# One-core tower of token mixer, linear attention and eight experts: attention by single rows in laps, its later steps set beside the experts, heads set in the layers

## The reference

```python
h = tok(x)      # embedding, decayed running sum over the sequence, norm;
                # 4 layers: x += gelu(LN(x) @ W1 + b1) @ W2 + b2   (128 -> 512 -> 128)
                # head: h = x @ head_W + head_b                    (128 -> 64)
h = h + attn(layernorm(h))
    # xn = rmsnorm(x); q, k, v = xn @ w_qkv (4 heads of 32)
    # q = softmax over the head's 32; k = softmax over the sequence and 4 memories
    # context = k v^T (32x32 a head); out = rmsnorm(context q @ w_out + b_out) + x
h = h + ffn(layernorm(h))
    # xn = LN(x); logits = xn @ Wr + br; top 2 of 8 experts, w = softmax of the two
    # y = sum over experts of w[e] * (gelu(xn @ W1[e] + b1[e]) @ W2[e] + b2[e])
```

## Time and profile before

| | |
|---|---|
| median of 3 runs | 480.24 us |
| profiled execution | 481.16 us, span 479.4 us |
| PE, DVE, ACT, POOL busy | 87%, 76%, 69%, 59% of the span |
| last matmul of the layers ends | 246.4 us |
| heads on PE | 249.3 to 262.1 us |
| last turn of attention begins | 343.0 us |
| first spread of gates | 381.5 us |
| last sum transposed | 474.5 us |

### The profile page before, as it was taken

How to read it: one execution, slowest core, us unless ns; L and a number is a source line. 1 busy time by engine, 2 the same in 40 slices (tenths; PEclk the granted TensorE clock), 3 DMA queues, 4 the chain that set the end, 5 groups by cost and what they waited for, 6 DMA issues and landing times.

```text
span 479.4 us, 6268 instructions
## 1 busy us (share of the span) xinstructions
PE 414.8 (87%) x1965; PEld 333.3 (70%) x1965; DVE 364.4 (76%) x925; ACT 328.8 (69%) x530; POOL 282.1 (59%) x416
## 2 busy tenths in 40 slices
PE   3765799999999999999999495959593989999995
PEld 2653678888888888887779384848472767777773
DVE  4996489999999999999849759697937756666662
ACT  1255588888888888888961534444463689999893
POOL 0267467777777777778005916464642066677763
PEclk9999799999999999999995768687675699999997
DMA  6700021221222222222000000000000000000000
GB/s 219 267 1 1 1 44 43 46 46 45 43 49 43 44 50 44 45 44 45 23 1 1 0 2 1 1 1 1 1 0 1 1 1 12 11 12 12 11 12 22
DMA packets 15833, 14.93 MB, mean 31 GB/s; under 512 B 9781, under 2 KB 10553, under 8 KB 15545
## 3 DMA queue, kind: packets, MB, share of 16 engines
q1 hardware_dynamic: 15800, 14.54, 12.8%
HBM read 13.42 MB, written 1.11 MB: 30 GB/s over the span
## 4 chain that ended last, share of the span: by engine, by line
PE 36%; DVE 32%; ACT 23%; POOL 4%; issue 4%; DMA 0%; POOLq 0%; SPq 0%; DVEq 0%; ACTq 0%
PE ps L1223 31%; DVE hid_lo L868 7%; ACT hid L562 7%; ACT hid_hi L567 6%; DVE stats L790 6%; DVE xn L858 6%; ACT xn_hi L558 4%; PE ps L1421 2%; DVE hh L1042 1%; DVE x L802 1%; PE ps L1534 1%; ACT x L600 1%; DVE x L809 1%; DVE st L1029 1%; POOL xn_hi L493 1%
## 5 line engine op out<-in xcount | busy, mean ns | idle before, releaser
L868 DVE TENSOR_TENSOR hid_lo<-hid,hid_hi 128x1024 fp32r<-128x1024 f32 x64 | 78.3, 1223 | 23.0 <-ACT hid_hi L567 23.0
L562 ACT ACTIVATE hid<-ps,b_fold 128x512 f32<-128x512 f32 x128 | 83.9, 682 | 15.9 <-PE ps L1223 15.8
L1223 PE MATMUL ps<-xn_hi,w_all 128*128 128x512 f32 x256 | 89.0, 409 | 0.9 <-DVE xn_lo L863 0.9
L1223 PE MATMUL ps<-hid_hi,w_all 128*128 128x512 f32 x256 | 84.1, 390 | 0.0
L567 ACT ACTIVATE hid_hi<-hid 128x1024 fp32r<-128x1024 f32 x64 | 67.9, 1061 | 2.0
L1198 DVE TENSOR_TENSOR hid<-hid,ps 128x512 f32<-128x512 f32 x64 | 43.8, 686 | 33.1 <-ACT hid L710 31.6
L1223 PEld LDWEIGHTS ps<-xn_hi,w_all 128*128 128x128 f32 x256 | 48.7, 190 | 12.8 <-DVE xn_lo L863 2.2
L1223 PEld LDWEIGHTS ps<-hid_hi,w_all 128*128 128x128 f32 x256 | 48.1, 188 | 10.3 <-DVE hid_lo L868 0.4
L1223 PE MATMUL ps<-xn_lo,w_all 128*128 128x512 f32 x128 | 50.4, 394 | 0.0
L1223 PE MATMUL ps<-hid_lo,w_all 128*128 128x512 f32 x128 | 49.8, 389 | 0.0
L710 ACT ACTIVATE hid<-ps,eb_fold 128x512 f32<-128x512 f32 x64 | 43.6, 686 | 8.1 <-PE ps L1223 7.5
(11 more groups left out here) (221 smaller groups left out, 890.9 us busy)
## 6 DMA issues: line engine op xcount, KB each, us to landing
rstd_row<-roots SPq DMA_DIRECT2D x29, 256.0 KB, 4.1
hh<-in_tokens SPq DMA_DIRECT2D x8, 256.0 KB, 8.1
hid<-in_w SPq DMA_DIRECT2D x2, 1024.0 KB, 9.0
out<-hh SPq DMA_DIRECT2D x8, 128.0 KB, 2.0
ew_raw<-in_expert_w SPq DMA_DIRECT2D x1, 512.0 KB, 9.5
roots<-rstd SPq DMA_DIRECT2D x29, 2.0 KB, 1.4
ew_raw<-in_expert_w SPq DMA_DIRECT2D x1, 256.0 KB, 9.4
cons<-in_constants SPq DMA_DIRECT2D x1, 233.0 KB, 2.7
```

The costliest lines, as they stand in the source:

```text
L562: act.activation(hid[:, j % 2, f, :], bank[f], ACT.Gelu, bias=b1_fold[:, j // B * F + f:j // B * F + f + 1]).then_inc(gelu_done, 1)
L868: dve.tensor_tensor(hid_lo[:, j % 2, 2 * p:2 * p + 2, :], hid[:, j % 2, 2 * p:2 * p + 2, :], hid_hi[:, j % 2, 2 * p:2 * p + 2, :].bitcast( ...
L1223: return pe.matmul(out, lhsT, rhs, start=start, stop=stop)
```

## The change

1. *Late weights in the layers.* The fold's matmuls go into the prologue (`late_folds`), ACT's gains and hi parts to the start of rows j = 5 to 19, DVE's lo parts to the end of rows j = 6 to 24; the zeroing of w_pad on POOL goes between two roots.
2. *Heads in the layers.* `head(0)` to `head(4)` stand in rows j = 27 to 31 on PE, with `head_out` and `head_moments` on DVE one row later, and the rest behind; the z of row 0 is made and transposed ahead of the last `down`. Two banks serve the heads instead of four.
3. *Attention by single rows in laps.* Lap m runs from -9 to 7; those from 0 on are the expert rows. In lap m row m+9 gets its products and exps, row m+8 its K transposes and context, row m+6 its Q transposes and attend, row m+5 its output norm and residual, row m+4 its expert z and router columns; pairs of rows get gates. q stays in x for all rows, mx_sb has 4 places, qT and ezf are tiles of their own.
4. *Z by tensor operations.* `z_of` and `expert_z` take the whole row (128x256) with broadcast mean and root instead of four pieces with scalars; POOL subtracts the mean for z.
5. *Router.* The sum of the two logit parts is made by PE (`logits` multiplies by the selection matrix), the top two for 2 rows at once (128x64), the gate weights by total and gap (4 operations), the factor 0.5 in ACT's copy.
6. *Experts.* Hidden units turn through 2 banks instead of 4 (the other two carry the laps' transposes and products); the steps of rows 4 to 7 stand between the units, on each engine at a fixed u = n % 8.

The diff, cut to its core (ACT's steps between the experts' units stand like PE's: `q_turned` u=1, `ez_hi` 2, `attended` 4, `expert_z_turned` 5, `logits_out` 7, `copy_gates` 3 or 7):

```diff
 HALF = B // 2
 W1_STEP = 6
-GATES_BANK = (4, 6, 7, 4, 7, 7, 7, 7)
-LOGITS_BANK = (0, 5)
-HEAD_BANK = (2, 3, 6, 7)
-Z_ROW = 4
+HEAD_BANK = (7, 6)
+HIDDEN_BANK = (0, 4)
+SPREAD_BANK = (2, 3)
+EARLY_HEADS = 5
...
+def turning_bank(lap):
+    return 1 if lap >= 0 else 4 * (lap % 2) + 2
+def product_bank(lap):
+    return 5 if lap >= 0 else 4 * (lap % 2) + 3
...
+            for m in range(FIRST_LAP, 0):
+                a = m - FIRST_LAP
+                if m + 5 >= 0:
+                    output_norm(m + 5, (m + 5) % 2)
+                if a + 2 < B:
+                    roots_of(a + 2)
+                    centred(a + 2)
+                if a + 1 < B:
+                    residual_base(a + 1)
+                if m + 5 >= 0:
+                    expert_norm(m + 5, (m + 5) % 2)
...
             for n in range(UNITS):
-                if n % E in LO_BY_POOL:
+                m, u = divmod(n, E)
+                if u == 0 and m + 5 < B:
+                    output_norm(m + 5, (m + 5) % 2)
+                if u in LO_BY_POOL:
                     hidden_lo(n)
+                if u == 6 and m + 5 < B:
+                    expert_norm(m + 5, (m + 5) % 2)
...
             for j in range(L * B):
+                if j == 5:
+                    projection_scale()
+                if j == 7:
+                    projections_hi()
+                if j in (9, 11):
+                    expert_scale((j - 9) // 2)
+                if j in (13, 15):
+                    first_layer_hi((j - 13) // 2)
+                if j == 17:
+                    second_layer_hi()
+                if j == 19:
+                    expert_bias_hi()
                 for f in range(F):
...
+            for m in range(FIRST_LAP, 0):
+                a, c = m - FIRST_LAP, m - FIRST_LAP - 1
+                if a < B:
+                    z_turned(a, a % 2)
+                if m == FIRST_LAP:
+                    act.preload_act_table(ACT.Exp)
+                if m == -1:
+                    act.preload_act_table(ACT.Gelu)
+                if c >= 0:
+                    k_turned(c, c % 2)
+                if m + 6 >= 0:
+                    q_turned(m + 6, m % 2)
+                if m + 4 >= 0:
+                    ez_hi(m + 4, m % 2)
+                if m == -1:
+                    gate(0)
+                if a < B:
+                    exp_k(a, a % 2)
+                if a + 1 < B:
+                    z_hi(a + 1, (a + 1) % 2)
+                if m + 6 >= 0:
+                    attended(m + 6, m % 2)
+                if a < B:
+                    exp_q(a, a % 2)
+                    copy_v(a, a % 2)
+                if m + 4 >= 0:
+                    expert_z_turned(m + 4)
+                    logits_out(m + 4)
+                if m == -1:
+                    copy_gates(0)
...
+                if j >= L * B - 4:
+                    head_out(j - (L * B - 4))
                 if j == 0:
                     x_lo(1)
                 h_lo(j, 0)
+                if j >= L * B - 4:
+                    head_moments(j - (L * B - 4))
                 if 0 < j < L * B - 1:
                     x_lo(j + 1)
                 h_lo(j, 1)
+                if j == 6:
+                    gate_rows()
+                if j == 8:
+                    output_weights()
+                if j == 10:
+                    projections_lo()
+                if j in (16, 18):
+                    first_layer_lo((j - 16) // 2)
+                if j == 20:
+                    second_layer_lo()
+                if j == 21:
+                    v = expert_bias_lo()
+                if j == 22:
+                    v = expert_bias_gap(v)
+                if j == 23:
+                    v = expert_bias_half(v)
+                if j == 24:
+                    expert_bias(v)
+                if j == L * B - 2:
+                    z_of(0, 0)
             residual(L * B - 2)
+            z_lo(0, 0)
+            head_out(4)
+            head_moments(4)
             residual(L * B - 1)
...
+            for m in range(FIRST_LAP, 0):
+                a, c = m - FIRST_LAP, m - FIRST_LAP - 1
+                if c >= 0:
+                    v_total = softmaxes(c, c % 2)
+                if m + 5 >= 0:
+                    output_moments(m + 5, (m + 5) % 2)
+                if m == -2:
+                    v = first_max(0)
+                if a < B:
+                    max_k(a, a % 2)
+                    negated(a % 2, own.n)
+                if m == FIRST_LAP:
+                    for b in range(5, B):
+                        head_out(b)
+                if a + 1 < B:
+                    z_of(a + 1, (a + 1) % 2)
+                if m + 4 >= 0:
+                    expert_z(m + 4, m % 2)
+                if m == -2:
+                    v = first_hot(0, v)
+                if m == -1:
+                    v = weights(0, v)
+                    gates_out(0, v)
+                if c >= 0:
+                    masked_context(c, c % 2)
+                if a < B:
+                    max_q(a, a % 2)
+                    sub_q(a, a % 2, own.n)
+                if a + 1 < B:
+                    z_lo(a + 1, (a + 1) % 2)
+                if m + 4 >= 0:
+                    expert_z_lo(m + 4, m % 2)
+                if c >= 0:
+                    scaled_m(c, c % 2, v_total)
+                if a < 3:
+                    head_moments(a + 5)
+                if m + 5 >= 0:
+                    scaled_output(m + 5, (m + 5) % 2)
+                    residual_moments(m + 5, (m + 5) % 2)
+                if m == -2:
+                    v = second_max(0, v)
+                    v = second_hot(0, v)
...
+                m, u = divmod(n, E)
                 if n < UNITS:
                     dve_job(n)
                 if 1 <= n <= UNITS and (n - 1) % E in LO_BY_DVE:
                     hidden_lo(n - 1)
-                if n % E == SKEW + 2 and n >= E:
-                    output(n // E - 1)
+                if u == 0 and m + 5 < B:
+                    output_moments(m + 5, (m + 5) % 2)
+                if u == 1 and m + 4 < B:
+                    expert_z(m + 4, m % 2)
+                if u == 3 and m + 4 < B:
+                    expert_z_lo(m + 4, m % 2)
+                if u == 4 and m + 5 < B:
+                    scaled_output(m + 5, (m + 5) % 2)
+                if u == 5 and m + 5 < B:
+                    residual_moments(m + 5, (m + 5) % 2)
+                if m % 2 == 0 and m < 6:
+                    if u == 2:
+                        v = first_max(m // 2 + 1)
+                    if u == 3:
+                        v = first_hot(m // 2 + 1, v)
+                    if u == 6:
+                        v = second_max(m // 2 + 1, v)
+                    if u == 7:
+                        v = second_hot(m // 2 + 1, v)
+                if m % 2 and m < 6:
+                    if u == 2:
+                        v = weights((m + 1) // 2, v)
+                    if u == 3:
+                        gates_out((m + 1) // 2, v)
+                if u == SKEW + 2 and n >= E:
+                    output(m - 1)
...
             for j in range(L * B):
                 if j + 3 < L * B:
                     turn(x[:, (j + 3) % B, :], x_ready, j + 4, j + (B + 3))
                 if j + 1 < SPREAD_BY_PE:
                     broadcast((j + 1) % 4, j + (B + 1))
                 up(j)
+                if j == L * B - EARLY_HEADS:
+                    pe.wait_ge(ld["headw"], 16)
+                    pe.wait_ge(normed, B + SPREAD_BY_PE + FREE)
+                if j == L * B - EARLY_HEADS + 1:
+                    pe.wait_ge(stats_ready, B * (L + 1) + FREE)
+                if j >= L * B - EARLY_HEADS:
+                    head(j - (L * B - EARLY_HEADS))
                 if j:
                     down(j - 1)
-            down(L * B - 1)
...
                 pe.wait_ge(zt_ready, b + 1)
+                if b >= 2:
+                    pe.wait_ge(m_ready, b - 1)
                 mm(kb, wqkv[:, 0, P:2 * P], zt[:, k, :], stop=False)
                 mm(kb, wqkv[:, 1, P:2 * P], zt[:, k, :], start=False).then_inc(k_done, 1)
+                wait_turned(turned)
+                wait_products(products)
...
+            head(5)
+            for m in range(FIRST_LAP, 0):
+                a, c = m - FIRST_LAP, m - FIRST_LAP - 1
+                turned_by_now, products_by_now = dict(turned), dict(products)
+                if 0 < a < B:
+                    z_transposes(a, a % 2)
+                if c >= 0:
+                    k_transposes(c, c % 2)
+                if m + 6 >= 0:
+                    pe.wait_ge(qsub_ready, c + 1)
+                    pe.wait_ge(v_ready, c + 1)
+                    q_transposes(m + 6, m % 2)
+                if m == -2:
+                    logits(0)
+                if a < B:
+                    qkv(a, a % 2, turned_by_now, products_by_now)
+                if m == FIRST_LAP:
+                    head(6)
+                    head(7)
+                    pe.wait_ge(h0_ready, B)
```

(54 more changed lines are left out.)

764 lines of the change are left out of this document (332 added, 432 removed).

## The result

The changed kernel takes 469.03 us (median of 5 runs, 467.92 to 476.24) where the kernel before takes 480.24 (479.58 to 484.65). The ratio is 0.9736, with a 95% interval of 0.9691 to 0.9781: 2.2 to 3.1% faster. The forecast was 456.5 with a range of 446 to 471, so direction and range hold, and the gain is 11.2 us where 23.8 stood. Its stages come out the same within 0.7 us in a second profile (experiment 1).

What follows compares the result with a forecast made beforehand. Bound: PE and an equal ACT-DVE chain in the layers, no full engine between, PE in the experts. 481.16 + 1.2 + 5.5 + 4.5 + 1.5 - 51.6 + 15.1 = 457.4 us profiled, 456.5 as median; range 446 to 471.

Steps and rivals of the forecast that it cites:

- Prologue, +1.2: Prologue: 18 small fold matmuls moved into PE's step 5 cost 1.2 us, bounds 0 and 2.3.
- Layers and heads, +5.5, +4.5, +1.5: Layers: DVE's weight splits and POOL's memset cost 5.5 us, five heads 4.5, z_transposes(0) ahead of the last down 1.5.
- the 263: Sign: last down of the layers at 259 us, right between 256 and 263; a layer end past 263 is wrong.
- Laps, 83.5: Between layers and experts: single-row laps take 83.5 us where 135.1 stood, -51.6, from 76.8 at full and 88.9 at half clock.
- The clock rival: Laps: every lap costs its half-clock length and the experts start cold, 464 us in all; chance 0.18.
- The experts, +15.1: Experts: PE's added steps, less gate transpositions already there, plus 5 us for stalls and the half-clock start: +15.1 us.
- PE's added steps: Experts: transpositions, attends, routes, logits and gates add 12.1 us to PE at full clock, less 2.1 already there.
- the 5: Experts: 5 us for stalls in rows 0 to 3 and the start at the half clock, bounds 0 and 12.
- DVE 13.3 against PE 14.6: Experts, row 0: busy sums of 14.6 us for PE, 13.3 for DVE, 12.7 for ACT, 10.7 for POOL.
- DVE and POOL slow each other: Laps and expert rows 0 to 3: DVE work beside POOL's gets longer, +7 and +6, 470 us; chance 0.1.
- Lock-step: Expert rows 0 to 3: two hidden banks make each unit a chain of 1.9 us, not 1.7; 467 us; chance 0.1.

Runs made afterwards that it cites:

- experiment 1: The changed kernel run again with no edit, for a second profile and time: ratio to the kernel before 0.9687 to 0.9848 (interval).
- ez_later: Changed kernel with PE's expert z transpositions at unit 5 instead of 4 and the route at unit 7 instead of 6: ratio 0.9634 to the kernel before.
- before_again: The kernel before, run again with no edit, for a second profile of its prologue: the layers began at 59.1 us; no total time given.
- ez_folds: ez_later with the prologue's late folds moved behind the first weight split and DVE's two additions ahead of the layers: ratio 0.9612 to the kernel before.
- ez_one_input: ez_later and one_input together on the changed kernel: 117.1 us from first spread to last sum in the experts; no total time given.
- one_input: Changed kernel with POOL's two-input subtraction for the hidden low halves replaced by a one-input multiplication, sums less exact: 465.56 us against 473.54 unedited.

## Why the prediction was right in sign and wrong in size

By its own terms, against the profiled executions:

*Prologue, +1.2.* 3.3 to 4.0. The bounds were 0 and 2.3, and the step failed where I took half of the 18 matmuls' time as hidden and nothing for what stands behind them. Even at the higher pace, where they take the 2.3 that I had, the layers begin 3.3 to 4.0 later, with the broadcast and transpositions behind them at the lower pace; at the lower pace the matmuls themselves take nearly twice as long.

*Layers and heads, +5.5, +4.5, +1.5.* In sum 11.5 forecast, 9.5 to 9.9 measured. Split: the memset 0.1 instead of 1.6, the experts' splits 2.2 instead of 2.7, which leaves 7.2 to 7.6 for heads, z transpositions and the other splits, where 7.2 stood. The layers' end is at 265, past the 263 that I had named as a sign of error, but that comes from the later begin, 62.2 instead of 54.3.

*Laps, 83.5.* 78.1 to 83.8 in twelve profiles, 81.4 in the first. The sum is right, and DVE as the bound of the later laps, but its parts erred in opposite ways: DVE is busy 66.9 us where the nine laps were to hold 70.9, at a granted clock of 0.84 where 0.72 was taken, and waits 14.6 where 12.6 was left. The clock rival (every lap at the half level) did not come.

*The experts, +15.1.* +31, and this step failed. Between the sums stand 17.4, 16.9, 17.0, 12.6, 13.5, 11.3 and 9.2 us, where I had 14.5, 14, 13, 12.5, 11.5, 11.5 and 11.0, and 26.1 from the first spread to the first sum instead of 17.0 before. The forecast was 10.0 for PE's added steps (12.1 - 2.1) and 5 for everything else: stalls and the start at the half clock. It is the 5 that failed; it measured 19.8.

(a) The added steps take 11.4, counted in the profile of `ez_later` from each start to the next and less the gate transpositions that stood there before. The logits are the piece that was mis-sized, 5.6 in all instead of 2.7: each pair needs 16 small instructions,

```profile
341.51 1.95 PE L1327 MATMUL ps<-cons,xn 16*128 16x8 f32 x16
```

where the kernel before had 8 transpositions a pair. A product with the selection matrix is an fp32 matmul, and shows as two instructions each. The other added steps take 5.7 where 7.3 stood.

(b) PE's own work in the experts is stretched. With the two moves of `ez_later`, near the full clock, PE is busy 106.6 against 88.8 (`before_again`), +17.8, which is 6.4 more than the added steps. Most of it stands in the matmuls with the experts' weights, the same in both kernels, at 0.99 and 1.00 of the clock; first `ez_later`, then `before_again`, those matmuls alone:

```profile
340.20:458.40 118.20, 78.50 (x253) 44.98 (x252) 0.00 (x0) 0.00 (x0) 0.99 0.04 9
386.70:479.40 92.70, 73.68 (x249) 43.48 (x248) 0.00 (x0) 0.00 (x0) 1.00 0.05 11
```

Waits too short to show as idle are the likely reason; no run here shows it.

(c) The clock: 3.7 us of PE's time at the lower level (2.3 by `ez_folds`), for which only the start was counted. (d) Idle PE: 13.6 against 3.9, +9.7. Together 11.4 + 6.4 + 3.7 + 9.7 = 31.2.

The idle part was forecast from busy sums a row, DVE 13.3 against PE 14.6, so DVE seemed to have room. (ACT and POOL stand in that sum at 9.3 and 7.7, where the stage's busy time gives 9.6 and 7.3; it changes nothing.) What failed in it: DVE's steps were priced at their lengths without POOL, though half of them read two SBUF operands beside POOL's subtractions; and no step asked whether an input that PE needs at unit 4 is made by DVE before unit 4. A sum over a row can't show that. These two causes are shown, and are worth 6.8 to 7.1 us together (`ez_one_input`, `one_input`), POOL's longer instruction included. The larger part of the excess stays open: `ez_later` still has PE idle for 11.6 us, waiting for several others in short pieces (us in total, times, longest, over its experts):

```profile
PE ps L1327 <- POOL xn_lo L516: 3.4, 6, 0.9
PE ps L1327 <- DVE hid L1276: 2.7, 6, 0.9
PE ps L1327 <- ACT hid_lo L723: 2.5, 3, 1.5
```

*The rivals.* "DVE and POOL slow each other" is the one that came, at 0.1 in my chances, in the experts and not in the laps, where POOL's instructions are short. Its price was taken from the earlier trace rows, 2.62 against 1.86, a factor of 1.4; an operation that starts just behind POOL's has a factor of 3.6 (1.52 against 0.42). The Trainium skill, "SBUF — State Buffer", section "SBUF: two separate sides", calls it an exclusive lock for the whole instruction, taken by DVE operations with two SBUF inputs; the trace agrees for POOL's subtraction (0.81, 1.52). Beside POOL's one-input instruction of 1.5 us, which reads SBUF too, DVE was held up only in the first 0.5 us (0.65 and 0.85, against 0.23 and 0.42 for later starts), so there the lock didn't last for the whole instruction. "Lock-step" (each unit of rows 0 to 3 a chain over the two hidden banks) had its sign, PE waiting for the gates' product; a single misplaced step explains 4.6 to 5.7 us of that. No run had four hidden banks, so this rival stands untested for the rest.

The net: 2.1 more in the prologue, 2 less in the layers, 2 less in the laps and 16 more in the experts make 14 where 12.5 us lie between the 456.5 forecast and 469.0. The remaining 1.5 is less than laps and prologue vary by. That the time lies in the range at all is in part luck: the term for stalls had bounds of 0 and 12 and measured 19.8, and the laps and layers came out 2 us lower each.

## What to carry to other kernels

When work is moved beside a pipelined loop, check each new step of an in-order engine against the unit at which its input is made, in the order of the other engine, before summing busy times: one transposition placed a unit too early cost 4.6 to 5.7 us here, and moving it back cost nothing. Price a DVE operation with two SBUF inputs beside a two-input operation of POOL by what is left of POOL's instruction plus its own length, and prefer PSUM or single inputs for what must slip between. And count a stall of PE at more than its length: the clock behind it cost as much again in one profile here (2.3 and 2.3 us) and nearly twice as much in another (2.0 and 3.7).

## What the runs showed of the hardware that was not expected

- A DVE tensor_tensor of 128x64 with two SBUF inputs takes 0.22 us alone, 0.81 when it starts 0.54 us into a 1.28 us POOL subtraction, and beside a one-input POOL tensor_scalar of 1.5 us 0.65 when it starts 0.04 behind POOL's start, 0.23 when it starts 0.54 behind. With one PSUM input, and in reductions and batch-norm steps, it isn't held up.
- Splitting POOL's subtraction of 1.28 us into four mostly takes 1.7 to 1.9 us and shortens the wait only to the current piece (0.41).
- PE's pace in the prologue changes at 19 to past 34 us of the span in executions of the same code, transpositions going from 1.12 to 0.66 us, and the begin of the layers moves by 6 us with it (53.1 and 59.1 in the kernel before), while the clock column shows 1.00 in both up to 40 us. Behind 18 small matmuls (64x1 and 64x8) set into the prologue at step 5 the transpositions took 1.06 in all nine profiles, in six of them after 0.66 ahead of the matmuls.
- Behind 4 us in which PE worked 1.53, it was granted 0.50 for 5 us of uninterrupted work.
